# Last stage of a routed feed-forward kernel: adds given to GpSimd, rows loaded in eight pieces, results stored in smaller pieces

## The reference

```python
x2 = x + _layernorm(attn(_layernorm(x)))             # "x after attention"
xn = _layernorm(x2)
shared = silu(xn @ sw_gate) * (xn @ sw_up) @ sw_down
probs  = softmax(xn @ router_w.T)                     # 8 experts
top_w, top_i = top_k(probs, 2); top_w /= sum(top_w)
routed = sum over the 2 chosen experts of top_w * expert(xn)
y   = routed + sigmoid(xn @ shared_gate_w)[:, None] * shared
out = x2 + _layernorm(y)                              # mean and variance over 256 features
```

## Time and profile before

| | us |
|---|---|
| runs (3): lowest, median, highest | 618.31, 619.25, 620.9 |
| span of the profiled execution, first to last instruction | 617.5 |
| TensorE matmul busy | 530.9 (86%) |
| VectorE busy | 410.8 (67%) |
| ScalarE busy | 261.6 (42%) |
| GpSimd busy | 111.8 (18%) |
| mean granted TensorE clock | 0.923 |

### The profile page before, as it was taken

How to read it: one execution, slowest core, us unless ns; L and a number is a source line. 1 busy time by engine, 2 the same in 40 slices (tenths; PEclk the granted TensorE clock), 3 DMA queues, 4 the chain that set the end, 5 groups by cost and what they waited for, 6 DMA issues and landing times.

```text
span 617.5 us, 8177 instructions
## 1 busy us (share of the span) xinstructions
PE 530.9 (86%) x2464; PEld 419.4 (68%) x2464; DVE 410.8 (67%) x1249; ACT 261.6 (42%) x465; POOL 111.8 (18%) x133
## 2 busy tenths in 40 slices
PE   2844358999659999999999998999998989999991
PEld 1423135577546677887678786888886889999870
DVE  6786744779874699885488793341839656766447
ACT  4720355616364524266531435311144556666304
POOL 1510003200001404001305000022005114444400
PEclk9976778999767999999899999699998989999997
DMA  8970100001010003021001010001007224454263
GB/s 287 422 204 3 33 2 0 1 0 35 34 34 1 0 2 104 1 68 35 0 1 69 2 35 34 1 26 44 34 1 265 61 61 123 121 139 122 77 258 136
DMA packets 29549, 44.42 MB, mean 72 GB/s; under 512 B 3211, under 2 KB 24203, under 8 KB 29163
## 3 DMA queue, kind: packets, MB, share of 16 engines
q1 hardware_dynamic: 24515, 32.95, 16.8%
q0 software_dynamic: 3408, 9.38, 4.1%
q10 hardware_dynamic: 1584, 1.57, 0.9%
HBM read 27.55 MB, written 16.34 MB: 71 GB/s over the span
## 4 chain that ended last, share of the span: by engine, by line
PE 69%; DVE 20%; ACT 5%; issue 2%; DMA 2%; POOL 0%; ACTq 0%; POOLq 0%; DVEq 0%; SPq 0%
PE psum L765 14%; PE psum L724 12%; PE psum L725 12%; PE psum L726 12%; PE psum L791 6%; PE psum L840 3%; PE psum L734 3%; PE psum L812 2%; PE psum L826 1%; DVE XC L1214 1%; PE psum L915 1%; PE psum L932 1%; PE psum L962 1%; DVE rt L1001 1%; DVE rt L1000 1%
## 5 line engine op out<-in xcount | busy, mean ns | idle before, releaser
L634 ACT ACTIVATE SM<-psum 128x512 f32<-128x512 f32 (+1 forms) x56 | 33.1, 595 | 132.9 <-PE psum L726 94.9
L1340 DVE TENSOR_TENSOR SM<-SM,psum 128x512 f32<-128x512 f32 (+1 forms) x56 | 38.2, 682 | 45.8 <-ACT SM L634 45.4
L510 POOL DMA_INDIRECT x_dispatched<-XN,dest x32 | 34.8, 1087 | 167.2 <-DVE XN L1408 158.7
L765 PE MATMUL psum<-WOU,SM 128*128 128x256 f32 x256 | 60.0, 379 | 0.2 <-DVE SM L1340 0.2
L791 PE MATMUL psum<-WQKV,HT 128*128 128x512 f32 (+1 forms) x128 | 53.0, 568 | 6.1 <-ACT QKV L569 2.7
L501 POOL TENSOR_TENSOR OG<-QKV,hvec 128x256 f32<-128x256 f32 x16 | 13.3, 834 | 237.2 <-ACT IG L576 220.0
L765 PEld LDWEIGHTS psum<-WOU,SM 128*128 128x128 f32 x256 | 48.2, 189 | 10.8 <-issue 3.4
L519 POOL DMA_INDIRECT y_routed<-GO,g_dest x39 | 37.9, 971 | 64.2 <-ACT GO L699 63.4
L791 PEld LDWEIGHTS psum<-WQKV,HT 128*128 128x128 f32 x128 | 27.4, 220 | 29.6 <-issue 23.6
L765 PE MATMUL psum<-SDN,SM 128*128 128x256 f32 (+1 forms) x192 | 45.0, 383 | 0.0
L765 PEld LDWEIGHTS psum<-SDN,SM 128*128 128x128 f32 (+1 forms) x192 | 36.1, 191 | 7.0 <-issue 1.3
(11 more groups left out here) (285 smaller groups left out, 1350.7 us busy)
## 6 DMA issues: line engine op xcount, KB each, us to landing
XG<-x_dispatched SPq DMA_DIRECT2D x39, 130.0 KB, 2.6
YF<-y_routed SPq DMA_DIRECT2D x4, 1024.0 KB, 9.0
RUPR<-rup SPq DMA_DIRECT2D x1, 2816.0 KB
X<-x SPq DMA_DIRECT2D x4, 512.0 KB, 6.3
x_after_attention<-X SPq DMA_DIRECT2D x4, 512.0 KB, 2.8
QKV<-x ACTq DMA_DIRECT2D x3, 512.0 KB, 3.6
y_shared<-SH SPq DMA_DIRECT2D x3, 512.0 KB, 2.9
SHF<-y_shared SPq DMA_DIRECT2D x1, 1536.0 KB
```

The source lines that it names most:

```text
L510: nc.gpsimd.indirect_dma_start(XD[:, :], bass.IndirectOffsetOnAxis(dest[:, i, old + j:old + j + 1], 0), XN[:, j, :], None).then_inc(dispat ...
L634: nc.scalar.activation(SM[0:rows, g % 3, 0:tb], p_pair(n)[0][0:rows, 0:tb], ACT.Silu).then_inc(silu_ready, 1)
L765: last = nc.tensor.matmul(p_down[:, j // 2, (j % 2) * D:(j % 2 + 1) * D], SM[0:rows, g % 3, j * P:(j + 1) * P], weight[0:rows, m, :], star ...
L1340: nc.vector.tensor_tensor(SM[0:rows, g % 3, 0:tb], SM[0:rows, g % 3, 0:tb], value_rows(n, rows)[:, 0:tb], ALU.mult).then_inc(hid_ready, 1)
```

## The change

SP loads the rows in eight pieces of one pair each. For each pair GpSimd adds the second routed rows of the even tile to its first ones, in place in YF, and counts `rows_added`; TensorE adds both halves of the odd tile and one half of the even tile, and counts `sum_psum` once per pair. The eight result adds of tiles 0 to 7 go from VectorE to GpSimd (`out_first`), behind its row adds; those of tiles 8 to 15 stay (`out_last`). The first half is stored in two pieces of four tiles, as before, the second in four pieces of two. In the diff, names of semaphores that are only declared are left out.

```diff
-QUARTER = NT // 4
+PAIRS = NT // 2
...
-            def quarter_rows(dram, i):
-                return dram[i * QUARTER * P:(i + 1) * QUARTER * P, :].rearrange("(j p) d -> p j d", p=P)
-
-            for i in range(4):
-                q = slice(i * QUARTER, (i + 1) * QUARTER)
-                pairs = YD[2 * q.start * P:2 * q.stop * P, :].rearrange("(j p k) d -> p j (k d)", p=P, k=2)
-                sp.dma_start(YF[:, q, :], pairs).then_inc(yf_in[i], 16)
-            for i in range(4):
-                sp.wait_ge(out_ready, (i + 1) * QUARTER)
-                sp.dma_start(quarter_rows(out, i), x_tiles(i * QUARTER, QUARTER)).then_inc(stored, 16)
-            sp.wait_ge(stored, 16 * 4)
+
+            for k in range(PAIRS):
+                pairs = YD[4 * k * P:4 * (k + 1) * P, :].rearrange("(j p k) d -> p j (k d)", p=P, k=2)
+                sp.dma_start(YF[:, 2 * k:2 * k + 2, :], pairs).then_inc(yf_in[k], 16)
+
+            def store(n, count):
+                sp.dma_start(out[n * P:(n + count) * P, :].rearrange("(j p) d -> p j d", p=P), x_tiles(n, count)).then_inc(stored, 16)
+
+            for n in range(0, FIN[0], 4):
+                sp.wait_ge(out_first, n + 4)
+                store(n, 4)
+            for n in range(FIN[0], NT, 2):
+                sp.wait_ge(out_last, n - FIN[0] + 2)
+                store(n, 2)
+            sp.wait_ge(stored, 16 * (FIN[0] // 4 + FIN[1] // 2))
...
+            for k in range(PAIRS):
+                pool.wait_ge(yf_in[k], 16)
+                rows = YF[:, 2 * k, :]
+                nc.gpsimd.tensor_tensor(rows[:, 0:D], rows[:, 0:D], rows[:, D:2 * D], ALU.add).then_inc(rows_added, 1)
+            pool.wait_ge(xf_in, 16)
+            for n in range(FIN[0]):
+                pool.wait_ge(fin_normed, n + 1)
+                x = x_tiles(n, 1)[:, 0, :]
+                nc.gpsimd.tensor_tensor(x, x, sh_tile(n), ALU.add).then_inc(out_first, 1)
...
             for n in range(NT):
                 add_to_tile(n, sh_tile(n), start=n % 2 == 0, stop=False)
-            for n in range(NT):
-                if n % QUARTER == 0:
-                    pe.wait_ge(yf_in[n // QUARTER], 16)
+            for k in range(PAIRS):
+                pe.wait_ge(yf_in[k], 16)
                 for i in range(2):
-                    last = add_to_tile(n, YF[:, n, i * D:(i + 1) * D], start=False, stop=i == 1)
-                last.then_inc(sum_psum, 1)
+                    add_to_tile(2 * k + 1, YF[:, 2 * k + 1, i * D:(i + 1) * D], start=False, stop=i == 1)
+                pe.wait_ge(rows_added, k + 1)
+                add_to_tile(2 * k, YF[:, 2 * k, 0:D], start=False, stop=True).then_inc(sum_psum, 1)
...
             def finish(n):
                 dve.wait_ge(fin_normed, n + 1)
                 x = x_tiles(n, 1)[:, 0, :]
-                nc.vector.tensor_tensor(x, x, sh_tile(n), ALU.add).then_inc(out_ready, 1)
+                nc.vector.tensor_tensor(x, x, sh_tile(n), ALU.add).then_inc(out_last, 1)
...
-            dve.wait_ge(xf_in, 16)
             for g in range(len(FIN)):
                 nj = FIN[g]
                 r, shift = fin_r[:, g % 2], fin_n[:, g % 2]
                 for j in range(nj):
-                    dve.wait_ge(sum_psum, (FSTART[g] + j) // 2 * 2 + 2)
+                    dve.wait_ge(sum_psum, (FSTART[g] + j) // 2 + 1)
                     step(nc.vector.bn_stats(fst[:, j, :], f_tile(FSTART[g] + j)))
-                    if g > 0 and j < FIN[g - 1]:
-                        finish(FSTART[g - 1] + j)
                 settle()
                 aggregate(nj, (fst, fmv, va))
                 link(rsqrt(r[:, 0:nj], *scratch(nj)))
```

More of the change, by code:

```diff
@@ L309, in build @@
             sem, ("lmax_ready", "exp_ready", "picked", "rank_psum", "shared_gate"))
-        x2_ready, x2_kept, sh_ready, sh_kept, out_ready = map(sem, ("x2_ready", "x2_kept", "sh_ready", "sh_kept", "out_ready"))
+        x2_ready, x2_kept, sh_ready, sh_kept, rows_added, out_first, out_last = map(
+            sem, ("x2_ready", "x2_kept", "sh_ready", "sh_kept", "rows_added", "out_first", "out_last"))
         before_ready, tok_iota, slot_iota, base_iota, pad_zero, pad_ready, pads_kept = map(
@@ L317, in build @@
                   "gdest_ready", "gw_ready"))
-        xf_in, sf_in, yf_in = sem("xf_in"), sem("sf_in"), [sem(f"yf_in{i}") for i in range(4)]
+        xf_in, sf_in, yf_in = sem("xf_in"), sem("sf_in"), [sem(f"yf_in{i}") for i in range(PAIRS)]
         sum_psum, fin_stats, fin_normed = map(sem, ("sum_psum", "fin_stats", "fin_normed"))
```

## The result

| | before | changed |
|---|---|---|
| median of 4 runs each, us | 619.64 | 616.67 |
| lowest to highest, us | 618.31 to 620.9 | 616.35 to 616.9 |
| span of the profiled execution, us | 617.5 | 615.2 |
| first row load issued, us from the start | 584.27 | 584.75 |
| from there to the end of the span, us | 33.2 | 30.5 |

The ratio is 0.995, with a 95% interval from 0.9935 to 0.9965: 3.0 us faster. The median of before is now 619.64, with a fourth run, and was 619.25 when the prediction was made. The work ahead of the first row load is the same in both kernels, but in the thirteen traces of this study it ended between 582.4 and 585.4 us.

A forecast was written before the change was run, and what follows sets the result against it. TensorE's 16 adds bound the first half, VectorE alone the second. ScalarE's second start 2.3 us earlier and 0.67 us less store gave 614.5 against a 617.5 span, -3.0; on the 619.25 median, 616.2 us, range 613.2 to 618.6.

The forecast's parts named there:

- Part 1: Rows in eight pieces, one add in four moved from TensorE: pair 3 read at 594.4 instead of 597.10, 2.7 us earlier.
- the last rival: Row loads: each new border costs what a lone load costs, 1.8 us; 619.5 us, chance 0.06.
- the estimate that takes the pieces in series: Row loads: some 2 us per transfer, so 8 us for four more pieces, slower than before.
- Part 2: VectorE's small operations get through one per GpSimd instruction; in the first chain this costs 1.3 us.
- Part 3: First-half result adds moved to GpSimd: 2.9 us removed from VectorE's second statistics, 1.95 us paid back in its second chain.
- Part 4: Final stores: halving a 0.52 MB store saves 0.67 us, so the tail is 2.5 us instead of 3.20.
- The rival of little contention: VectorE's small operations slip by between GpSimd's instructions: -6.3 us, 613.0 us; chance 0.16.
- the rival of more contention: VectorE's aggregation held too, GpSimd at 0.80 us, longest holds in first chain: -0.4 us, 618.8 us; chance 0.15.
- GpSimd as the bound: GpSimd's adds become the bound: no change at 1.1 us each; at 1.66 us, 627 us; chance 0.06.

The follow-up runs named there:

- stores of four: Changed kernel with the second half stored in two pieces of four tiles, as before; 617.08 us, ratio 0.9972.
- quarter loads: Changed kernel with four row loads of four tiles instead of eight; 616.93 us, ratio 0.9972.
- adds outside the chains: Changed kernel, GpSimd row adds for pairs 0 to 4 only, result adds of tiles 4 to 7 on VectorE behind second chain; 612.87 us, again 612.68.
- row adds for five pairs: Changed kernel with GpSimd row adds only for pairs 0 to 4, TensorE doing all adds of pairs 5 to 7; 614.99 us, ratio 0.9935.
- results only: Changed kernel with only the result adds moved: four row loads, all row adds on TensorE, stores of four tiles; 619.11 us, ratio 1.0010.

## Why the prediction was right

On the clock of before, the forecast and the trace stand like this.

| step | forecast | measured |
|---|---|---|
| GpSimd's eight row adds start, us | 588.3 to 598.15 | 588.3 to 598.2, none off by over 0.31 |
| a GpSimd add, us | 0.73, pitch 0.69 | 0.72, pitch 0.69 |
| statistics of pair 3 | 594.4 | 594.4 |
| holds in the first chain | 3 operations, 1.3 us | 3, 1.24 us |
| ScalarE's first start | 599.8 | 599.8 |
| statistics of the second group | 2.8 us | 2.74 us |
| GpSimd's last result add ends | 606.0 | 606.3 |
| holds in the second chain | 5 operations, 1.95 us | 5, 2.2 us |
| ScalarE's second start | 607.75 | 607.97 |
| last add to the end | 2.5 us | 2.55 us |
| end of the span | 614.5 | 614.7 |
| median, us | 616.2 | 616.67 |

Of the 0.47 us between the two medians, 0.39 are the rise of the median of before from 619.25 to 619.64.

**Part 1** held to 0.1 us where it matters. The four new borders cost nothing in rate: from 589.0 us on, the busy times by stretch of the changed kernel (last number: GB/s) show the rate of before.

```profile
589.00:591.80 2.80, 2.61 (x12) 1.79 (x11) 0.91 (x3) 0.00 (x0) 1.20 (x2) 1.00 1.00 377
591.80:594.50 2.70, 2.53 (x11) 2.08 (x12) 1.38 (x4) 0.00 (x0) 1.44 (x2) 1.00 1.05 394
594.50:597.40 2.90, 2.90 (x14) 2.09 (x13) 2.31 (x14) 0.00 (x0) 1.45 (x2) 1.00 1.02 375
```

One gap between pieces was longer than the others, 1.92 us from the row add at 590.07 to that at 591.99, and the pieces after it came 1.3 to 1.4 us apart. That also disposes of the last rival, and of the 8 us of the estimate that takes the pieces in series: the last row add starts at 598.2 on the clock of before. **Part 2**, one VectorE operation per GpSimd add, was read from two rows of block 0 and decided the size of the result: of the 6.3 us that the edits freed, 3.5 were paid back (1.24 + 2.22). Kernels with fewer adds and with more adds moved as it says, in the number of holds. One step of it was right by luck: it left aggregation uncharged because a reduction with one SBUF input had kept its time. One input isn't the reason, since the TENSOR_SCALAR operations of the same rows and of these chains have one and are held. **Part 3** was 0.2 us short, because GpSimd started its first result add 0.37 us later than taken. **Part 4** is confirmed by the stores of four.

The rival of little contention fell with the five long operations in a row; in the traces shown one operation of a chain slipped, with the first add after a pause (quarter loads). Aggregation wasn't held, GpSimd kept to its pitch, so the rival of more contention didn't occur either. GpSimd as the bound would have needed 1.1 us an add; it took 0.72. What the prediction left out is that a result add costs 0.48 us when GpSimd does it beside the chain and 0.37 when VectorE does it itself ((5.72 - 2.74) / 8): five of the eight moved adds cost more on the engine they were moved to. The version with the adds outside the chains follows from that line.

## What to carry to other kernels

A chain of small dependent VectorE operations on SBUF advances one operation per GpSimd instruction while GpSimd reads SBUF, here those with two inputs and the TENSOR_SCALAR ones with one alike; so before moving work to GpSimd, count how many of its instructions fall beside such a chain, and price each at its pitch less one free operation. In this kernel work moved to GpSimd paid beside statistics from PSUM and aggregations, and the rest did better on VectorE in a place where it waits for another engine. When an effect is smaller than the variation of what runs ahead of it, measure from a common event in the traces.

## What the hardware showed unasked

- GpSimd's first result add began 0.47 us after ScalarE's first result in the changed kernel, 1.9 us after its last row add, and 0.14 us after it where GpSimd had been idle for 4.3 us (row adds for five pairs) or 19.2 us (results only). No run tells why; it stays open.
- With the same columns as both operands, a GpSimd add of 128x256 took 0.57 us, with two different ones 0.69; a memset of 128x512 0.47.
